# A language-model block on one core: TensorE takes the attention's units two at a time

## The chip, the cores and the metric

The kernel runs on one NeuronCore of a Trainium2 chip. The time is the device time of one execution in microseconds (us), from the chip. The median of three executions of the kernel before is 593.24 us (589.75 to 594.96). One further execution was profiled; it took 594.88 us.

## The reference

Rows of a table are gathered by token, an attention over each sequence is added, and then a mixture of experts:

```python
h = take(tok_weight, x)                      # x: 32 x 128 tokens, D = 256
X = layernorm(h)
q, k, v = X @ Wq, X @ Wk, X @ Wv             # 16 heads of 16
scores = where(causal, q @ k.T / 4, -inf)
h = h + (softmax(scores) @ v) @ Wo           # attention over 128 positions, all heads
X = layernorm(h)
top1 = argmax(softmax(X @ wg))               # 8 experts; capacity 641 rows each
y = gelu(X[slots] @ W1[e] + b1[e]) @ W2[e] + b2[e]     # 256 -> 1024 -> 256
h = h + where(valid, y[slot], 0) * weight_of_top1
```

All arrays are float32.

## The kernel before, in words

Two phases follow each other on the same core: attention with routing (to about 317 us of the profile), then the eight experts (to the end). The change is in the first.

**Groups and units.** The 32 sequences are taken in 16 groups of two (NG = 16, GB = 2). The attention of one group is eight units (UNITS = 8): a unit is four heads of one of the two sequences. For each unit there are, in this order: scores S (four 128 x 128 bf16 products, PE line 726, into bank S0 or S1 by the unit's parity), their row maxima on DVE (line 919, `mx`); once all eight maxima of a group are there, PE turns them (line 788, into bank M2), ACT negates them into `nm` (line 600) and sends them by a DMA (line 604) as one more row of `qs`; then the shifted scores C (four products with 97 contraction rows, line 739, into bank C0 or C1), the exponential on ACT (line 534, into `pt`, four buffers), the causal mask on POOL (line 479), and the values PV (line 833): eight matmul records, four heads in two passes each, each head in its own 32 columns of the array, into bank PV, which holds four units. ACT copies bank PV out after four units (`os`, line 544).

**Steps.** All engines go through 21 steps, i = 0 to 20, written out, with eight places s = 0 to 7 in each. Work of different groups overlaps by fixed lags: at place s the unit of S is (s - 12) mod 8, that of C (s - 23) mod 8, that of PV (s - 25) mod 8; so a unit's PV stands two places after its C. Besides these, some places hold other work, which the change calls `rest`:

- s = 1: projection Q of group i (`project`, twelve products, line 687), and ranks of the router (lines 810 to 814)
- s = 2: turn of `os` of the second sequence of group i - 4 (line 708, bank M1), projection K of group i (bank M2)
- s = 3: turn of `on` (line 629, bank M1), after DVE's division (lines 940, 942)
- s = 4: turn of the maxima of group i - 2 (line 788)
- s = 5: output projection O of group i - 4 (line 687, twelve products of 264 columns, banks M1 and M2); it waits for `otl` of DVE and, since it writes M2, for ACT's `nm`
- s = 6: turn of `os` of the first sequence of group i - 3 (line 708, bank M0)
- s = 7: value projection of group i, first sequence; turn of the normalised rows `xn` of group i + 1 (line 629, bank M0), which waits for DVE's division out of M0; value projection of the second sequence

At every place of step i the order on PE is: filler products (`idle_work`, only in a few steps at the start and the end), S, C, the rest, PV.

**Waits that matter.** S of unit u waits for the maxima of unit u - 2 (two S banks). C of unit u waits for the exponential of unit u - 2 (two C banks). C of a group's first unit (s = 7) waits for the DMA of `nm`. PV of unit u waits for the mask of unit u; the first PV of each four waits for the copy `os` of the four before.

**The other engines' order is written out too.** DVE: maxima of place s, then that place's other work: at s = 1 the ranks (`place`) and the rest of Q (`qr`, line 933), at s = 2 the division and the rest of K (`kr`, line 933, after ACT's copy of K, line 551), at s = 3 `otl`, at s = 5 the addition of O's result (line 977), the router's terms and the normalisation, at s = 6 a division and statistics. ACT: exponential of place s, then copies; at s = 4 the exponential, then `nm` and the issue of its DMA; at s = 5 the exponential, then `os`.

Of the kernel before, what the change touches and what calls it, by code (L numbers as in the profile page):

```python
# [35 lines left out]
UNITS = 8  # L36
# [25 lines left out]
def wait(engine, semaphore, value):  # L62

    if isinstance(value, int) and value <= 0:
        return
    engine.wait_ge(semaphore, value)
# [107 lines left out]
def attention_phase(nc, sb_in, sem, v):  # L174
    x, table, wq, wk, wv, wo, wg, b1, b2 = (v[n] for n in ("x", "table", "wq", "wk", "wv", "wo", "wg", "b1", "b2"))
    NB, S, D, E, H, DK, CAP, KC, GB, NG, GT, QUADS = (
        v[n] for n in ("NB", "S", "D", "E", "H", "DK", "CAP", "KC", "GB", "NG", "GT", "QUADS"))
# [3 lines left out]
    bS, bC, bPV, bM0, bM1, bM2 = (v[n] for n in ("bS", "bC", "bPV", "bM0", "bM1", "bM2"))  # L181
# [9 lines left out]
    with ExitStack() as scope:  # L191
# [96 lines left out]
        def group(n, off):  # L288

            if isinstance(n, int) and not 0 <= off < NG:  # L290
                return None
            return Turn(n, off, RING)
# [4 lines left out]
        def steps(eng, step):  # L297
            for i in range(LAST):
                step(0, i)
# [5 lines left out]
        def shift_unit(n, i, s, lag):  # L305

            d, u = divmod(s - lag, UNITS)
            return group(n, i + d), u
# [314 lines left out]
        def tensor(pe):  # L623
# [9 lines left out]
            def idle_work(bank, count):  # L633

                for _ in range(count):
                    pe.matmul(bank[:, :], trib[:, :], constb[:, :, :], start=True, stop=True)

            FILL = {(1, 1): 6, (1, 4): 32, (2, 6): 8, (NG + 3, 1): 4, (NG + 3, 3): 3, (NG + 3, 5): 6, (NG + 3, 6): 3,
                    (NG + 3, 7): 6, (NG + 4, 1): 2, (NG + 4, 6): 2, (NG + 5, 1): 4}
# [64 lines left out]
            def turn_values(dst, g, b):  # L704

                wait(pe, a_os, g.times(GB, b + 1))
                for a in range(QUADS):
                    last = pe.transpose(dst[:, a * P:(a + 1) * P], osb[b][:, a, :], identf[:, :])  # L708
                last.then_inc(pe_OT, 1)

            def step(n, i):
                for s in range(UNITS):

                    idle_work(bPV if i < NG else bS[0], FILL.get((i, s), 0))
                    g, u = shift_unit(n, i, s, S_LAG)
                    if g:
                        if u == 0:
# [10 lines left out]
                                             ks[g.slot][:, hh, b * S:(b + 1) * S], start=True, stop=True)  # L728
                        last.then_inc(pe_S, 1)

                    g, u = shift_unit(n, i, s, C_LAG)
                    if g:
                        if u == 0:
# [7 lines left out]
                                             qs[g.slot][0:KS_ROWS + 1, hh, b * S:(b + 1) * S], start=True, stop=True)  # L741
                        last.then_inc(pe_C, 1)

                    g = group(n, i - 4)
                    if g and s == 2:
# [69 lines left out]
                    if g and s == 6:  # L817
# [2 lines left out]
                        wait(pe, v_on, g.times(GB, -1))  # L820
                        turn_values(bM0, g, 0)

                    g, u = shift_unit(n, i, s, PV_LAG)
                    if g:
                        b = u // QUADS
                        if u == 0:
                            wait(pe, a_V[1], g.times(1, 1))
                        if u % QUADS == 0:
                            wait(pe, a_os, g.times(GB, b))
                        wait(pe, p_sel, g.times(UNITS, u + 1))  # L830
                        for j in range(4):
                            hh = (u % QUADS) * 4 + j
                            last = pe.matmul(bPV[32 * j:32 * j + 32, (u % QUADS) * S:(u % QUADS + 1) * S],  # L833
                                             va[g.slot][:, b, hh, :], pt[u % 4][:, j, :], start=True, stop=True)
                        last.then_inc(pe_PV, 1)

            steps(pe, step)
            idle_work(bS[0], 44)

        def vector(dve):  # L840
# [207 lines left out]
            steps(dve, step)  # L1048

        return {"sync": sync, "gpsimd": gpsimd, "scalar": scalar, "tensor": tensor, "vector": vector}  # L1050


# [332 lines left out]
```

## Time and profile before

| | |
|---|---|
| median of three executions | 593.24 us |
| profiled execution, its own time | 594.88 us |
| its span | 593.1 us |
| mean granted TensorE clock | 0.978 |
| busy: PE, PE weight loads | 546.1, 471.0 us |
| busy: DVE, ACT, POOL | 403.3, 341.8, 264.6 us |

Busy time is the union of an engine's instructions over the span; a matmul's end is modelled, so neighbouring matmuls overlap, and the distance from one start to the next says what one costs. A bracket after a row, `[0.21 <-issue]`, is the idle time of that engine before it and what ended it.

### The profile page before, as it was taken

Reading aid. Unit: us, or ns where it says so; the run is one execution under the profiler, and the core shown is the slowest. Engines: PE = TensorE matmul, PEld = TensorE weight load, DVE = VectorE, ACT = ScalarE, POOL = GpSimd, SP = SyncE. Lnnn points to the kernel's source line nnn. Section 1 sums busy time; section 2 is a strip of 40 time slices with the busy share of each in tenths; the row PEclk is TensorE's granted clock in tenths of the full one; section 3 lists DMA queues with packets and bytes.
Section 4 is the critical chain, followed back from the end, with each engine's and each line's share of the span. In section 5 each row is a group of like instructions: output and inputs, shape, how many; then the busy total and the mean of one; then the engine's idle time right before and its main releaser. Section 6 shows DMA issues by size and latency. Waiting matters only on the chain.

```text
span 593.1 us, 13953 instructions
## 1 busy us (share of the span) xinstructions
PE 546.1 (92%) x5067; PEld 471.0 (79%) x5067; DVE 403.3 (68%) x1076; ACT 341.8 (58%) x760; POOL 264.6 (45%) x345
## 2 busy tenths in 40 slices
PE   6875889999999999998888899999999999999991
PEld 3654677777888887775553799999999999999990
DVE  7554689989999999988546475757475655666511
ACT  3422566666666666665423684858484948484820
POOL 6634777777676767765534004040302122121212
PEclk9998999999999999999789899999999999999996
DMA  3799867777777777671112701615050606020100
GB/s 111 209 259 290 260 231 232 236 242 238 234 216 225 228 238 220 193 240 67 39 45 81 216 1 38 190 34 195 24 201 18 206 12 194 30 71 8 30 5 27
DMA packets 44612, 86.51 MB, mean 146 GB/s; under 512 B 7615, under 2 KB 33780, under 8 KB 40897
## 3 DMA queue, kind: packets, MB, share of 16 engines
q1 hardware_dynamic: 37632, 72.83, 39.9%
q0 software_dynamic: 6144, 12.67, 6.8%
q8 instruction: 41, 0.67, 0.5%
q10 hardware_dynamic: 768, 0.13, 0.1%
q14 instruction: 27, 0.21, 0.1%
HBM read 52.64 MB, written 31.74 MB: 142 GB/s over the span
## 4 chain that ended last, share of the span: by engine, by line
PE 76%; DVE 8%; DMA 6%; issue 4%; POOL 4%; ACT 1%; POOLq 0%; SPq 0%; ACTq 0%; DVEq 0%
PE M L687 13%; PE PV L1276 10%; PE S L1259 10%; PE C L1259 10%; PE M L1276 9%; PE PV L833 6%; PE S L726 5%; PE C L739 4%; PE M L629 3%; DMA ks<-k_parts 2%; PE C L1226 2%; PE M L708 2%; PE M L1214 2%; DVE mx L919 1%; DMA k_parts<-kp 1%
## 5 line engine op out<-in xcount | busy, mean ns | idle before, releaser
L1137 POOL DMA_INDIRECT out_dram<-ys,xs x48 | 50.7, 1057 | 212.7 <-DVE ys L1328 202.9
L534 ACT ACTIVATE pt<-C 128x512 f32<-128x512 f32 x128 | 76.3, 596 | 73.7 <-PE C L739 66.1
L479 POOL TENSOR_SCALAR_AFFINE_SELECT pt<-pt 128x512 f32<-128x512 f32 x128 | 81.2, 638 | 46.7 <-ACT pt L534 45.8
L919 DVE TENSOR_REDUCE mx<-S 128x4 f32<-128x512 f32 x128 | 86.4, 681 | 11.1 <-PE S L726 9.4
L1341 DVE TENSOR_TENSOR hl<-gl,hh 128x324 fp32r<-128x324 f32 x128 | 63.3, 495 | 38.9 <-ACT hh L1177 32.0
L1177 ACT ACTIVATE hh<-gl 128x324 fp32r<-128x324 f32 x128 | 60.8, 482 | 0.0
L833 PE MATMUL PV<-pt,va 128*32 128x128 f32 x1024 | 55.2, 289 | 4.6 <-issue 2.9
L726 PE MATMUL S<-ks,qs 128*128 128x128 bf16 x512 | 50.7, 223 | 8.4 <-DMA ks<-k_parts 5.3
L726 PEld LDWEIGHTS S<-ks,qs 128*128 128x128 bf16 x512 | 29.4, 98 | 32.6 <-issue 25.9
L739 PE MATMUL C<-qs,ks 97*128 97x128 bf16 x512 | 50.8, 222 | 1.8 <-DMA qs<-nm 1.8
L1328 DVE SCALAR_TENSOR_TENSOR ys<-C,xs 108x256 f32<-108x256 f32 x48 | 21.8, 481 | 40.2 <-PE C L1226 37.1
L1183 ACT ACTIVATE gl<-S,biases 128x324 f32<-128x324 f32 x64 | 34.5, 541 | 15.4 <-PE S L1259 12.5
L1293 DVE TENSOR_TENSOR wel<-w_raw,weh 128x512 fp32r<-128x512 f32 x64 | 40.9, 684 | 0.7 <-issue 0.7
L1259 PE MATMUL S<-xh,weh 128*128 128x324 f32 x128 | 41.2, 322 | 0.0
L1276 PE MATMUL M<-hh,weh 128*128 128x324 f32 x128 | 41.1, 321 | 0.0
L1276 PE MATMUL PV<-hh,weh 128*128 128x324 f32 x128 | 40.4, 316 | 0.0
L1259 PE MATMUL C<-xh,weh 128*128 128x324 f32 x128 | 40.3, 315 | 0.0
L1259 PE MATMUL S<-xl,weh 128*128 128x324 f32 x128 | 39.9, 312 | 0.0
L1276 PE MATMUL M<-hh,wel 128*128 128x324 f32 x128 | 39.9, 312 | 0.0
L1259 PE MATMUL C<-xl,weh 128*128 128x324 f32 x128 | 39.9, 312 | 0.0
L1276 PE MATMUL M<-hl,weh 128*128 128x324 f32 x128 | 39.9, 311 | 0.0
L1276 PE MATMUL PV<-hl,weh 128*128 128x324 f32 x128 | 39.8, 311 | 0.0
(170 smaller groups left out, 1617.1 us busy)
## 6 DMA issues: line engine op xcount, KB each, us to landing
w_raw<-in_L_ffn_W_dram SPq DMA_DIRECT2D x32, 512.0 KB, 7.4
qs<-q_parts SPq DMA_DIRECT2D x48, 256.0 KB
ks<-k_parts SPq DMA_DIRECT2D x48, 256.0 KB
q_parts<-qp SPq DMA_DIRECT2D x16, 384.0 KB
k_parts<-kp SPq DMA_DIRECT2D x16, 384.0 KB
rows_of_slots<-w_raw SPq DMA_DIRECT2D x6, 877.5 KB, 8.4
xs<-rows_of_slots SPq DMA_DIRECT2D x7, 658.1 KB
out_dram<-h SPq DMA_DIRECT2D x16, 256.0 KB, 7.0
```

The costliest lines, as they stand in the source:

```text
L479: pool.affine_select(out=buf[:, :, :], in_=buf[:, :, :], compare_op=ALU.is_ge, fill=0.0, base=0, pattern=[[0, 4], [1, S]], channel_multipl ...
L534: act.activation(pt[u % 4][:, :, :], bC[u % 2][:, :].rearrange("p (j t) -> p j t", j=4), ACT.Exp, scale=SCALE).then_inc(a_exp, 1)
L687: last = pe.matmul(dst, lhs[a](k), rhs[b](k), start=(m == 0), stop=(m == len(pairs) - 1))
L726: last = pe.matmul(dst[:, j * S:(j + 1) * S], qs[g.slot][:, hh, b * S:(b + 1) * S], ks[g.slot][:, hh, b * S:(b + 1) * S], start=True, stop ...
L739: last = pe.matmul(bC[u % 2][:, j * S:(j + 1) * S], ks[g.slot][0:KS_ROWS + 1, hh, b * S:(b + 1) * S], qs[g.slot][0:KS_ROWS + 1, hh, b * S: ...
L833: last = pe.matmul(bPV[32 * j:32 * j + 32, (u % QUADS) * S:(u % QUADS + 1) * S], va[g.slot][:, b, hh, :], pt[u % 4][:, j, :], start=True, ...
L919: dve.tensor_reduce(mx[g.slot][:, 4 * (u % QUADS):4 * (u % QUADS) + 4, u // QUADS], bS[u % 2][:, :].rearrange("p (j t) -> p j t", j=4), AX ...
L1137: pool.indirect_dma_start(out=outf, out_offset=bass.IndirectOffsetOnAxis(ap=xs[e.slot][:, j, D + 3:D + 4].bitcast(U32), axis=0), in_=ys[j] ...
L1177: act.activation(hh[:, f, cols], gl[u % 4][:, :], ACT.Copy).then_inc(a_hh, 1)
L1259: last = pe.matmul(up_bank[u % 4][:, 0:NH], w1[a][:, k, f * P:(f + 1) * P], xt[b][:, k, half * NH:(half + 1) * NH], start=(m == 0), stop=( ...
L1276: last = pe.matmul(down_bank[v % 2][:, 0:NH], w2[a][:, c, d * P:(d + 1) * P], ht[b][:, c, half * NH:(half + 1) * NH], start=(m == 0), stop ...
L1341: dve.tensor_tensor(hl[:, f, cols], gl[u % 4][:, :], hh[:, f, cols].bitcast(F32), ALU.subtract).then_inc(v_hl, 1)
```

## The change

On PE alone, the attention's places are taken two at a time. For s = 0, 2, 4, 6: PV of s - 1 and s, S of s and s + 1, C of s and s + 1, then the rest of s, and the rest of s + 1. PV of s = 7 of a step thereby falls to the head of the next step. The fillers of s stand ahead of the pair, those of s + 1 between the two rests. No other engine's program changes, and the waits of each piece stay as they are.

```diff
             def step(n, i):
-                for s in range(UNITS):
-
-                    idle_work(bPV if i < NG else bS[0], FILL.get((i, s), 0))
+                def scores(s):
+
                     g, u = shift_unit(n, i, s, S_LAG)
...
                         last.then_inc(pe_S, 1)
 
+                def shifted(s):
+
                     g, u = shift_unit(n, i, s, C_LAG)
...
                         last.then_inc(pe_C, 1)
 
-
+                def rest(s):
 
                     g = group(n, i - 4)
...
                         turn_values(bM0, g, 0)
 
+                def weighted(s):
+
                     g, u = shift_unit(n, i, s, PV_LAG)
...
                         last.then_inc(pe_PV, 1)
+
+                for s in range(0, UNITS, 2):
+                    idle_work(bPV if i < NG else bS[0], FILL.get((i, s), 0))
+                    weighted(s - 1)
+                    weighted(s)
+                    scores(s)
+                    scores(s + 1)
+                    shifted(s)
+                    shifted(s + 1)
+                    rest(s)
+                    idle_work(bPV if i < NG else bS[0], FILL.get((i, s + 1), 0))
+                    rest(s + 1)
```

## Rows read from the trace of the kernel before

**Rows 1.** Page's totals; window: PE, PEld, DVE, ACT, POOL (instructions), PEclk, DMA, GB/s.

```profile
PE 546.1 (92%) x5067; PEld 471.0 (79%) x5067; DVE 403.3 (68%) x1076; ACT 341.8 (58%) x760; POOL 264.6 (45%) x345
...
200.00:220.00 20.00, 19.96 (x259) 16.26 (x257) 18.51 (x60) 13.58 (x34) 14.29 (x20) 1.00 0.86 258
```

**Rows 2.** The chain of waits (start us, us, what): O of steps 4, 8, 15.

```profile
81.82 1.71 PE M L687 x12
...
147.83 1.69 PE M L687 x12
...
257.72 1.72 PE M L687 x12
```

**Rows 3.** Timeline of PE (start us, us), places 2 to 5 of a late step.

```profile
205.17 0.61 PE L708 MATMUL M<-identf,os 128*128 128x128 f32 x4
205.54 0.37 PE L687 MATMUL M<-xth,wh 128*128 128x256 f32 x1
...
206.92 0.28 PE L687 MATMUL M<-xth,wl 128*128 128x256 f32 x1
207.13 0.43 PE L833 MATMUL PV<-pt,va 128*32 128x128 f32 x8
...
207.73 0.39 PE L739 MATMUL C<-qs,ks 97*128 97x128 bf16 x4
207.95 0.61 PE L629 MATMUL M<-identf,on 128*128 128x128 f32 x4
208.49 0.43 PE L833 MATMUL PV<-pt,va 128*32 128x128 f32 x8
208.85 0.40 PE L726 MATMUL S<-ks,qs 128*128 128x128 bf16 x4
209.08 0.39 PE L739 MATMUL C<-qs,ks 97*128 97x128 bf16 x4
209.31 0.27 PE L788 MATMUL M<-identf,mx 128*32 128x128 f32 x1
209.51 0.43 PE L833 MATMUL PV<-pt,va 128*32 128x128 f32 x8
209.87 0.40 PE L726 MATMUL S<-ks,qs 128*128 128x128 bf16 x4
210.10 0.39 PE L739 MATMUL C<-qs,ks 97*128 97x128 bf16 x4
210.51 0.36 PE L687 MATMUL M<-wh,oth 128*128 128x264 f32 x1
...
211.93 0.28 PE L687 MATMUL M<-wh,otl 128*128 128x264 f32 x1
```

**Rows 4.** Timeline of PE where two PV groups are neighbours.

```profile
302.31 0.64 PE L833 MATMUL PV<-pt,va 128*32 128x128 f32 x16
```

**Rows 5.** Timelines of ACT and DVE in the same step.

```profile
207.24 0.60 ACT L551 ACTIVATE kp<-M 128x512 bf16<-128x512 f32 x1 [0.40 <-PE M L687]
209.64 0.60 ACT L534 ACTIVATE pt<-C 128x512 f32<-128x512 f32 x1
210.12 0.25 ACT L600 ACTIVATE nm<-M 32x128 bf16<-32x128 f32 x1
...
207.87 0.69 DVE L933 TENSOR_TENSOR kr<-M,kp 128x512 f32<-128x512 f32 x1 [0.48 <-ACT kp L551]
208.48 0.68 DVE L919 TENSOR_REDUCE mx<-S 128x4 f32<-128x512 f32 x1
```

**Rows 6.** Timeline of PE and its weight loads: the turn of xn, same step.

```profile
215.25 0.42 PEld L629 LDWEIGHTS M<-identf,xn 128*128 128x128 f32 x4 [0.21 <-issue]
215.29 0.63 PE L629 MATMUL M<-identf,xn 128*128 128x128 f32 x4
```

**Rows 7.** The issues of line 604 by line: time to landing.

```profile
DMA to landing us min/median/max: 1.8/1.8/3.5
```

## The prediction

> **What bounds the kernel now.** I read the totals first. PE is busy for 546.1 of 593.1 us, and in a late window of the attention for 19.96 of 20.00 us, with DVE at 18.51 beside it, ACT at 13.58 and POOL at 14.29; the granted clock there is 1.00 [rows 1]. So PE sets the pace and DVE is close behind: neither has more than about 8% to give.
>
> Second, the chain of waits gives the period of a step. The twelve products of the attention's output projection (called O here, once in a step, at s = 5) stand in it at 81.82, 147.83 and 257.72 us [rows 2]. Between the first two lie four steps (66.01 / 4 = 16.50 us each), between the last two seven (109.89 / 7 = 15.70 us each). These are the twelve steps i = 4 to 15 that have all their work.
>
> Third, PE in order of time through half a step [rows 3], with the distances from start to start. Values (PV) to scores (S): 208.49 to 208.85, 0.36 us, and again 209.51 to 209.87. S to shifted scores (C): 0.23. C to a transpose: 0.22. A group of four transposes to PV: 0.54, to projection products: 0.37. A projection's last product to PV: 0.21. Two PV groups stand side by side once, at the attention's end: sixteen products last 0.64 where eight last 0.43, so the second group starts 0.21 after the first [rows 3, 4].
>
> Fourth, what DVE and ACT do between these products [rows 5], since the new order changes how much PE has between giving work away and needing its result.
>
> **The change, part by part.** It adds and removes no instruction; every matmul, copy and DMA stays. ACT's, DVE's, POOL's and SP's programs are untouched. So nothing is to be priced but edges between kinds of work on PE, and waits.
>
> *Edges.* Of the eight PV groups of a step, four now follow another PV. Each such pair costs 0.21 instead of 0.36 once: 4 x 0.15 = 0.60. An entry into PV is saved as well: after transposes 0.54 - 0.37 = 0.17 (the pair at s = 6), after C about half of that, 0.09, an estimate between 0 and 0.17 (the pair at s = 0), and nothing after projection products [rows 3, 4]. S after S and C after C are taken at 0.22, an estimate from S to C and C to a transpose (0.23, 0.22): the same four products stream in each. Sum: **-0.85 us a step**. Bounds: -0.6 (no entry saved) to -1.3 (all four saved at 0.17). In one sentence apart: the Trainium skill, TensorEngine Tiling (Array Packing), Key Properties, says that changing the tiling mode drains TensorE, and PV alone works in 32-column tiles here. By that rule alone the change is a gain; the trace agrees on the drain (0.36 against 0.21).
>
> *The fifth S (s = 5).* It needs the maxima of the third, which DVE makes only after the rest of K, which waits for ACT's copy of K: the last K product starts at 206.92, K's copy at 207.24, the rest at 207.87, the maxima run to 208.48 + 0.68 = 209.16 [rows 3, 5]. That is 2.24 us after the last K product. Today PE fills 2.95 us until the S at 209.87 (PV, S, C, transposes of `on`, PV, S, C, the transpose of the maxima, PV), so nothing waits. In the new order S and C of s = 3 have gone ahead of K, and between K's last product and the S of s = 5 only the transposes of `on`, two PV and one S are left: 0.22 + 0.54 + 0.21 + 0.36 + 0.22 = 1.55. **PE waits 2.29 - 1.55 = 0.74 us**, with 0.05 for the signal (an estimate; from `nm` to O it is 0.14), and the C of s = 4 stands behind that S, though its own inputs are there.
>
> *O behind the negated maxima.* O writes bank M2 and so waits for ACT's copy `nm` out of it, and ACT takes that copy after the exponential of s = 4. From the C of s = 4 (209.08) the exponential ends at 210.24, `nm` at 210.37, and O starts at 210.51: 1.43 us [rows 3, 5]. Today there stand the transpose of the maxima, PV, S and C between, 0.23 + 0.20 + 0.36 + 0.23 + 0.22 = 1.24, so PE waits 0.19. In the new order PV and S of that place are gone ahead: C 0.22, transpose 0.23, O 0.20 = 0.65. **The wait grows from 0.19 to 0.78, +0.59.**
>
> *The turn of the next rows (s = 7).* It needs bank M0, which DVE leaves after adding O's result, the router's terms, the normalised rows, a maxima and a division: O's last product is at 211.93, the turn at 215.29, and PE (its weight loads) is idle for 0.21 ahead of it, so this DVE chain already ends last [rows 3, 6]. Its 3.36 us stay. PE's own work between is 3.15 and shrinks by the pair at s = 6 (0.15 + 0.17) to 2.83: **the wait grows by 0.32.** In other words that pair's saving is eaten on the spot.
>
> Sum: 0.74 + 0.59 + 0.32 - 0.85 = +0.80. Today's 15.70 holds some small waits which the new ones cover, so I take **+0.7 us a step** in the seven late steps: 4.9. Walking once round the loop gives much the same: K's end to maxima to S, C, exponential, `nm`, O, addition, turn, values, and again to K, 16.4 us against 15.70.
>
> *Five further places.* (a) The early steps already take 16.50, 0.8 more than the late ones, so they already wait for DVE and ACT; the new loop of 16.4 us would fit in. Between 0 and +0.7 each; I take 0.2, nearer to 0 since 16.4 is under 16.50: 4 x 0.2 = 0.8. (b) Step 16 has no Q and K but still `nm` before O: +0.6, from the same rows. (c) The first steps have no O; the S wait of 0.74 and the saving of 0.85 cancel; the first transpose of the maxima comes one S later, +0.3. (d) The PV of an even s now needs the mask of a C that is nearer: where Q stands between (0.23 + 0.22 + 1.38 and more) it is hidden, in the last three steps without Q it may wait some tenths, against savings of the same size: 0, bounds -1 and +2. (e) The first C of a group moves ahead of the transposes at s = 6 and of an S. It needs the transfer of `nm`, issued as `nm` is done at 210.37, while O starts at 210.51; the C comes 1.42 + 0.22 + 0.21 + 0.36 + 0.22 + 0.23 + 0.22 = 2.9 after O's start, 3.0 after the issue [rows 3, 5]. The transfer lands after 1.8 in the median and 3.5 at most [rows 7]: hidden mostly, 0 taken, bound +0.5 a step.
> The expert phase runs the same program from the same signals: 0.
>
> 4.9 + 0.8 + 0.6 + 0.3 = **+6.6 us**. The profiled execution took 594.88 us (span 593.1), 1.64 above the median of 593.24, so 601.5 there and **599.8** against the median. Bounds of this case: saving 1.3 instead of 0.85 in twelve steps gives up to 5 less, though only where it is not in front of one of the three waits (S and turn each swallow one pair); the C wait and the early steps at their ends give 6 more. So 594 to 606.
>
> **The rivals.** *A: the saving counts, the waits don't.* Place: the twelve full steps, where PE shows no idle time to speak of. Price: 12 x -0.85 = -10, and 583 in the end. For it: PE 19.96 of 20.00 [rows 1], and the rule above. Against: the three paths are measured, not assumed, and O and the turn wait already today (0.19 and 0.21). It decides if the three waits together grow by less than 0.85 a step instead of 1.65, that is, if signals or the DVE place (0.48 idle before the rest of K) come out half as long. *B: a draw.* Waits and savings within 0.3 of each other in the late steps, nothing in the early ones: 591 to 597, about 594. For it: PE and DVE were both near full, and both orders serve the same DVE program. *C: a further wait.* The transfer of `nm` at over 3 us in most steps, or an ACT queue in which the exponential of s = 5 slips behind its issue and holds back the copy that the PV of s = 5 needs: +0.5 to +0.8 a step more, 608. For it: that copy is due within 0.1 us of its use in my walk; against: DMA lands in 1.8. That the change doesn't do what it says cannot be: the order on PE is its text.
>
> A last sentence on rules: the Trainium skill, TensorE: Matmul & The Clock Gate, Step-by-step, says that matmuls stay in program order and only weight loads are pulled ahead; by it a waiting S holds back all that stands behind, as today's wait before O shows (0.19, worked out above).
>
> **Numbers.** Forecast case 0.55, A 0.17, B 0.15, C 0.13. This kernel's measurement can tell about 1% (5.9 us) from no change. The forecast case is centred on 599.8 with 599.2 as the border, so half of it is slower (0.3 with its upper tail), half within 1% (0.25). With C, slower 0.43; with B, same 0.40; A gives faster 0.17. The range leaves out A and the tail of C: 590 to 607.
>
> **What would show it.** In the late steps O to O 16.4 instead of 15.70. PV pairs of 0.64 for sixteen. PE idle before the S of s = 5, released by DVE's maxima, about 0.7; before O, released by ACT's `nm`, about 0.8; before the turn of xn, released by `on`, about 0.5; PE's busy time per 20 us down to some 18. DVE idle before the rest of K of 0.7 or more. The forecast is wrong if the period falls below 15.5, or if PV to PV takes 0.36 as PV to S does (then slower still), or if C shows DMA as its releaser.

## The result and the profile after

| | before | changed |
|---|---|---|
| median (4 executions each) | 592.11 us | 617.78 us |
| lowest to highest | 589.75 to 594.96 | 614.72 to 620.6 |
| profiled execution, its span | 594.88, 593.1 | 620.6, 618.9 |
| mean granted clock | 0.978 | 0.952 |

The ratio is 1.043, 95% interval 1.0384 to 1.0475: 4.3% slower. The direction was forecast; the size (+25.8 us of span, against +6.6) was not, and the time lies outside the range.

The totals of the changed kernel (page, part 1), and then its busy time in 20-us windows (PE, PEld, DVE, ACT, POOL with their instructions, then granted clock, DMA share, GB/s), early and late in the attention. They answer [rows 1].

```profile
PE 547.4 (88%) x5067; PEld 484.8 (78%) x5067; DVE 403.1 (65%) x1076; ACT 345.8 (56%) x760; POOL 264.6 (43%) x345
```

```profile
80.00:100.00 20.00, 16.75 (x201) 14.57 (x201) 15.50 (x46) 10.16 (x23) 13.55 (x18) 0.91 0.61 192
...
200.00:220.00 20.00, 18.59 (x255) 16.30 (x254) 18.09 (x59) 12.81 (x28) 12.63 (x19) 1.00 0.70 216
```

The busy totals have hardly moved; idle time has been added. O's start in each step, read from PE's timeline as in [rows 2], cuts the loss into stretches ("in the sum" is what the prediction took; a step is counted from its O to the next):

| stretch | before | changed | more | in the sum |
|---|---|---|---|---|
| start to O of step 4 | 81.82 | 83.91 | 2.1 | 0.3 |
| steps 4 to 8 | 66.0 (16.4, 16.4, 17.0, 16.3) | 75.0 (19.8, 19.8, 18.2, 17.1) | 9.0 | 0.8 |
| steps 8 to 15 | 109.9 (15.7) | 115.5 (16.3; the last 17.6) | 5.6 | 4.9 |
| steps 15 to 19 | 52.1 (13.5, 14.1, 13.2, 11.3) | 59.8 (17.0, 16.0, 14.1, 12.8) | 7.7 | 0.6 |
| O of step 19 to the end | 283.2 | 284.7 | 1.5 | 0 |

Two of the rows can't be put down to the order of the pairs. The way to O of step 4 takes between 80.4 (e9) and 86.1 us (e4, e16) in the experiments below. The way from O of step 19 to the end takes 282.8 to 283.8 in most of them and 284.8 to 285.0 in e4, e12, e14, e16 and e18, of which e12 and e18 are the kernel before but for small edits.

**Late steps** came out near the forecast (16.4 forecast, 16.3 measured). PE of the changed kernel in the half step that answers [rows 3] and [rows 6]:

```profile
204.16 0.66 PE L629 MATMUL M<-identf,on 128*128 128x128 f32 x4
204.74 0.64 PE L836 MATMUL PV<-pt,va 128*32 128x128 f32 x16
205.32 0.40 PE L725 MATMUL S<-ks,qs 128*128 128x128 bf16 x4
206.22 0.40 PE L725 MATMUL S<-ks,qs 128*128 128x128 bf16 x4 [0.50 <-DVE mx L934]
206.45 0.61 PE L740 MATMUL C<-qs,ks 97*128 97x128 bf16 x8
...
212.53 0.63 PE L629 MATMUL M<-identf,xn 128*128 128x128 f32 x4 [0.32 <-DVE on L957]
```

The pair of PV lasts 0.64 for sixteen, as in [rows 4]. The second S stands 0.90 after the first where 0.22 is its own length: it waits for the maxima, and C behind it. ACT and DVE in the same step, answering [rows 5]:

```profile
206.88 0.60 ACT L534 ACTIVATE pt<-C 128x512 f32<-128x512 f32 x1 [0.55 <-PE C L740]
207.37 0.25 ACT L600 ACTIVATE nm<-M 32x128 bf16<-32x128 f32 x1
...
204.87 0.69 DVE L948 TENSOR_TENSOR kr<-M,kp 128x512 f32<-128x512 f32 x1 [0.77 <-ACT kp L551]
205.48 0.68 DVE L934 TENSOR_REDUCE mx<-S 128x4 f32<-128x512 f32 x1
```

The chain of waits through this step (start us, us, what) shows what sets the period:

```profile
204.87 0.69 DVE kr L948
205.56 0.61 DVE mx L934
...
206.22 0.40 PE S L725 x4
206.61 0.24 PE C L740 x4
...
206.88 0.36 ACT pt L534
...
207.37 0.26 ACT nm L600
...
207.76 1.71 PE M L687 x12
...
210.52 0.65 DVE xn L898 x2
...
211.96 0.43 DVE on L957
...
212.53 0.63 PE M L629 x4
213.16 0.73 PE M L687 x6
213.89 0.57 PE PV L836 x16
214.46 0.55 PE S L725 x8
215.02 0.45 PE C L740 x8
...
219.08 1.44 PE M L687 x12
...
220.54 0.60 ACT kp L551
...
221.17 0.69 DVE kr L948
```

It is a loop through four instructions: the turn of `xn` (T), ACT's copy of K (k), DVE's rest of K (r), DVE's addition of O's result (h), and again T. I read their starts in every kernel; four links add up to the period. Any four instructions of a step would; what makes these a loop is that each waits for the one before or stands behind its engine's own work. ACT is idle before the copy of K until PE's product (0.70 in the changed kernel, 0.40 in [rows 5]), DVE before the rest of K until that copy (0.77 and 0.48), and PE or its weight loads before the turn (0.32 and 0.21). In between, DVE works without a marked gap in the kernel before; in the changed one it is idle once, 0.41 before h, for O's product.

| late step, us | T to k | k to r | r to h | h to T | sum |
|---|---|---|---|---|---|
| before | 7.6 to 7.8 | 0.61 to 0.63 | 4.4 | 3.04 | 15.63 to 15.81 |
| changed | 8.01 | 0.63 | 4.63 | 3.03 to 3.07 | 16.30 to 16.34 |

The last of the seven is 17.57, with an h to T of 4.30: there C of s = 7 waits 1.22 for the transfer of `nm`.

The kernel before ran round this loop too. Its PE looked full (19.96 of 20.00), and PE's work is the longest link (T to k), but PE was not the bound by itself: e7 below takes the waits before the second S out and PE's saving still doesn't come through.

**Early steps.** The timeline of POOL and PE of the changed kernel at the head of step 5, then windows of 2 us there (columns as above):

```profile
92.32 1.02 POOL L431 DMA_INDIRECT h<-in_L_tok_weight_dram,idt  x1 [0.19 <-issue]
93.64 0.95 POOL L431 DMA_INDIRECT h<-in_L_tok_weight_dram,idt  x1 [0.31 <-issue]
94.60 1.22 POOL L479 TENSOR_SCALAR_AFFINE_SELECT pt<-pt 128x512 f32<-128x512 f32 x2
...
93.30 0.43 PE L836 MATMUL PV<-pt,va 128*32 128x128 f32 x8
95.30 0.42 PE L836 MATMUL PV<-pt,va 128*32 128x128 f32 x8 [1.57 <-POOL pt L479]
95.66 1.03 PE L725 MATMUL S<-ks,qs 128*128 128x128 bf16 x8
```

```profile
92.00:94.00 2.00, 1.63 (x23) 1.26 (x21) 1.85 (x8) 1.80 (x6) 1.51 (x3) 1.00 0.97 385
94.00:96.00 2.00, 0.70 (x12) 0.51 (x13) 1.90 (x5) 0.17 (x1) 1.81 (x3) 0.91 0.71 242
96.00:98.00 2.00, 2.00 (x19) 2.00 (x17) 0.78 (x2) 0.84 (x2) 0.18 (x1) 0.50 0.05 16
98.00:100.00 2.00, 2.00 (x14) 2.00 (x13) 0.68 (x2) 0.27 (x1) 1.58 (x2) 0.73 0.00 0
```

PV of s = 2 now stands ahead of K and needs the mask of a C issued at the head of the step. That mask waits in POOL's queue behind a gather of the step before (a gather is two indirect DMAs, 1.0 us of POOL each). PE stands idle for 1.57 us, and after it the granted clock is 0.50, the level of 1.2 GHz: eight S products take 1.03 us instead of 0.62. The link T to k is 11.5 us in the two steps of 19.8 (8.3 to 8.9 before). The third of these steps is long for another reason: C of s = 7 waits 1.11 for the transfer of `nm`.

How much of this is the clock can be read in e6 (below), where the same wait stands in two steps in a row, once with the fall of the clock and once without:

```profile
94.33 0.47 PE L836 MATMUL PV<-pt,va 128*32 128x128 f32 x8 [1.57 <-POOL pt L479]
...
113.45 0.43 PE L836 MATMUL PV<-pt,va 128*32 128x128 f32 x8 [1.57 <-POOL pt L479]
```

```profile
96.00:98.00 2.00, 2.00 (x14) 2.00 (x13) 0.52 (x3) 1.11 (x2) 1.10 (x2) 0.50 0.04 12
...
114.00:116.00 2.00, 2.00 (x28) 2.00 (x26) 1.54 (x5) 1.12 (x2) 0.65 (x2) 1.00 0.48 166
```

The first of these steps takes 19.12 us, the second 17.56; T to k is 11.50 and 9.94. So the clock is worth 1.56 us of such a step, and the wait with the new order near K the other 1.2 over the 16.4 of before. The changed kernel has 0.68 more in r to h (4.63 against 3.95), which gives its 19.8.

**Last steps.** ACT and PE of the changed kernel at the head of step 16:

```profile
281.24 0.60 ACT L534 ACTIVATE pt<-C 128x512 f32<-128x512 f32 x1 [1.25 <-PE C L740]
281.73 0.48 ACT L579 ACTIVATE ex<-dl,h 128x8 f32<-128x8 f32 x2
282.11 0.58 ACT L544 ACTIVATE os<-PV 128x512 f32<-128x512 f32 x1
...
280.58 0.40 PE L725 MATMUL S<-ks,qs 128*128 128x128 bf16 x4 [0.18 <-DVE mx L934]
280.81 0.61 PE L740 MATMUL C<-qs,ks 97*128 97x128 bf16 x8
...
282.80 0.64 PE L836 MATMUL PV<-pt,va 128*32 128x128 f32 x16 [1.03 <-issue]
283.38 1.03 PE L725 MATMUL S<-ks,qs 128*128 128x128 bf16 x8
```

S of s = 1 waits 0.18 for the maxima, C of s = 0 stands behind it, its exponential follows C, and `os` stands behind this on ACT; PV of s = 1 needs `os`. In these steps there is no Q between C and the pair of PV, only five short products, so PE is idle for 1.03 us. The clock falls again: 0.50 in the windows from 284 to 290. Taken from O to O, the granted clock of these four steps is 0.80, 0.89, 0.74 and 0.77; it was 1.00, 0.94, 0.76 and 0.90 before.

### The profile page after: what moved, and what is told of

The parts are those of the page before. It is cut to its first block, busy times and chain, and to the rows that moved or that the text cites. A ratio compares the mean times of both kernels' runs of the same rounds, so it can differ in the third digit from the quotient of the medians.

```text
span 618.9 us, 13953 instructions
## 1 busy us (share of the span) xinstructions
PE 547.4 (88%) x5067; PEld 484.8 (78%) x5067; DVE 403.1 (65%) x1076; ACT 345.8 (56%) x760; POOL 264.6 (43%) x345
## 4 chain that ended last, share of the span: by engine, by line
PE 64%; POOL 9%; DVE 8%; DMA 7%; issue 6%; ACT 3%; POOLq 0%; SPq 0%; ACTq 0%
PE M L687 10%; PE S L1274 9%; PE M L1291 9%; PE PV L1291 9%; PE C L1274 9%; PE S L725 4%; PE C L740 3%; POOL h L431 3%; PE PV L836 3%; DVE mx L934 2%; POOL pt L479 2%; DMA qs<-nm 2%; POOL rows_of_slots L415 2%; PE M L708 2%; PE M L1229 2%
## 5 line engine op out<-in xcount | busy, mean ns | idle before, releaser
L534 ACT ACTIVATE pt<-C 128x512 f32<-128x512 f32 x128 | 74.5, 596 | 89.3 <-PE C L740 78.6
L479 POOL TENSOR_SCALAR_AFFINE_SELECT pt<-pt 128x512 f32<-128x512 f32 x128 | 80.4, 635 | 68.5 <-ACT pt L534 68.2
L725 PE MATMUL S<-ks,qs 128*128 128x128 bf16 x512 | 45.3, 230 | 17.6 <-DVE mx L934 10.5
L1192 ACT ACTIVATE hh<-gl 128x324 fp32r<-128x324 f32 x128 | 59.2, 469 | 0.0
L725 PEld LDWEIGHTS S<-ks,qs 128*128 128x128 bf16 x512 | 31.1, 102 | 33.5 <-issue 19.0
L836 PE MATMUL PV<-pt,va 128*32 128x128 f32 x1024 | 44.7, 288 | 10.8 <-POOL pt L479 5.5
L740 PE MATMUL C<-qs,ks 97*128 97x128 bf16 x512 | 43.5, 230 | 3.1 <-DMA qs<-nm 2.9
L836 PEld LDWEIGHTS PV<-pt,va 128*32 128x32 f32 x1024 | 24.4, 111 | 22.0 <-POOL pt L479 8.0
L1274 PE MATMUL S<-xh,wel 128*128 128x324 f32 x128 | 40.1, 313 | 0.0
L1291 PE MATMUL PV<-hh,wel 128*128 128x324 f32 x128 | 39.9, 311 | 0.0
```

The lines of the kernel that those rows point to most:

```text
L479: pool.affine_select(out=buf[:, :, :], in_=buf[:, :, :], compare_op=ALU.is_ge, fill=0.0, base=0, pattern=[[0, 4], [1, S]], channel_multipl ...
L534: act.activation(pt[u % 4][:, :, :], bC[u % 2][:, :].rearrange("p (j t) -> p j t", j=4), ACT.Exp, scale=SCALE).then_inc(a_exp, 1)
L725: last = pe.matmul(dst[:, j * S:(j + 1) * S], qs[g.slot][:, hh, b * S:(b + 1) * S], ks[g.slot][:, hh, b * S:(b + 1) * S], start=True, stop ...
L740: last = pe.matmul(bC[u % 2][:, j * S:(j + 1) * S], ks[g.slot][0:KS_ROWS + 1, hh, b * S:(b + 1) * S], qs[g.slot][0:KS_ROWS + 1, hh, b * S: ...
L1192: act.activation(hh[:, f, cols], gl[u % 4][:, :], ACT.Copy).then_inc(a_hh, 1)
L1274: last = pe.matmul(up_bank[u % 4][:, 0:NH], w1[a][:, k, f * P:(f + 1) * P], xt[b][:, k, half * NH:(half + 1) * NH], start=(m == 0), stop=( ...
```

## The experiments

All ratios are to the kernel before, run beside it, with 95% intervals. Steps are from O to O; "steps 4 to 8" are the four between the O of step 4 and that of step 8, "late" the seven after them, "last" the four after those. They are read from one profiled execution of each kernel.

**One half alone (e1, e2).**

```diff
 # e1: the loop over pairs
+weighted(s - 1); weighted(s)
+scores(s); shifted(s); rest(s); idle_work(...); scores(s + 1); shifted(s + 1); rest(s + 1)
 # e2
+scores(s); scores(s + 1); shifted(s); shifted(s + 1)
+rest(s); weighted(s); idle_work(...); rest(s + 1); weighted(s + 1)
```

> Only PV is paired (PV of s-1 and s at the head of the pair); S, C and the rest stay one place at a time, so the S wait on the late maxima is gone and the wait before O is about halved. Theory M (the missing 19 us come from the PV of an even s, whose mask is now too near behind its C: behind the gathers on POOL in steps 4 to 7, behind the exponential in the last steps, and the slower clock that the idle time brings): the mask is as near as in the changed kernel, so steps 4 to 7 stay at 18 to 20 us, the last steps stay long, only the late steps fall to about 15.3; ratio to before 1.02 to 1.03. Theory L (the loop maxima, exponential, nm, O is what costs, everywhere): ratio 1.00 or below.

> Only S and C are paired; each PV stays alone at the end of its place, as before. Theory M: PV has its old distance to its mask, so steps 4 to 7 take about 16.5 us and the last steps as before; the waits for the maxima (about 0.6) and for nm (about 0.4) stay and no edge is saved, so late steps take 16.3 to 16.5; ratio 1.01 to 1.015. Theory L: all the loss is here, ratio 1.04 or more.

Measured: e1 600.19 us, 1.0097 (1.006 to 1.0135); steps 4 to 8 16.95 three times and 16.5, late 15.3 to 16.1, last 14.2, 14.4, 13.6, 11.2. e2 613.51, 1.0273 (1.0207 to 1.0339); steps 4 to 8 16.6 to 17.0, late 16.4 to 16.7 but for one of 19.7 and one of 18.2, last 14.2, 15.6, 13.7, 11.9; T to k 8.04. More of the loss comes with S and C in pairs than with PV. In e2's two long steps C of s = 7 waits 1.80 and 1.78 for the transfer of `nm`, a wait that no late step of the kernel before shows.

Neither half has the 19.8. Theory M had the wait right and its price wrong: in e1 PV of s = 2 waits 1.38 for its mask, nearly as long as in the changed kernel (1.57), but the clock stays at 1.00 and the step takes 16.95. The step of 19.8 needs the wait and the fall of the clock after it.

**More room for the mask (e3, e4).**

```diff
 # e3, POOL
-                    if isinstance(n, int) and gathers and i and s in (6, 7):
+                    if isinstance(n, int) and gathers and i and s == 6:
 # e4: PV pair behind the two C
+scores(s); scores(s + 1); shifted(s); shifted(s + 1); weighted(s - 1); weighted(s); rest(s); ...
```

> The changed kernel with one gather of a group (two indirect DMAs) a step on POOL, at s = 6, in twelve steps instead of two a step (s = 6 and 7) in six. Theory M: POOL is free for the mask at the head of the next step, PV of s = 2 doesn't wait 1.6 us, the clock stays at 1.00 from 80 to 140 us, steps 4 to 7 fall from 19.8 to about 16.4; ratio 1.02 to 1.03. Theory L: nothing changes, 1.04.

> The changed kernel with the pair of PV behind the two C instead of ahead of the two S: the saving of the pairs is kept and PV's mask gets 0.9 us more. Theory M: steps 4 to 7 fall below 18 us, in the last steps each pair waits about 0.9 less; late steps stay at about 16.3, since the loop over maxima, exponential and nm doesn't run through PV; ratio 1.015 to 1.025. Theory L: 1.04 as before, or more, as S waits longer for the maxima.

e3: 616.54, 1.0355 (1.0295 to 1.0415). The first two of steps 4 to 8 fall from 19.8 to 16.45 and 16.47, with the clock at 1.00: the gather at s = 7 was the early loss, as expected. But the next two take 18.0 and 19.4 instead of 18.2 and 17.1, the late ones 16.9 to 17.6 instead of 16.3 and the last of them 18.5, and most is given back. Part of that is the transfer of `nm`, for which C waits 1.65, 1.24 and 1.59 in three of these steps. e4: 644.85, 1.0785 (1.0695 to 1.0875), late steps 18.4 and more. Theory M missed; theory L had "or more, as S waits longer". PE of e4:

```profile
189.39 0.50 PE L740 MATMUL C<-qs,ks 97*128 97x128 bf16 x4 [2.33 <-DMA qs<-nm]
...
203.16 0.40 PE L725 MATMUL S<-ks,qs 128*128 128x128 bf16 x4 [1.35 <-DVE mx L934]
```

With S and C one PV pair sooner after K and O, S waits 1.35 for the maxima (0.50 in the changed kernel), and C of s = 7 waits up to 2.33 for the transfer of `nm`.

**The two waits (e5 to e8).**

```diff
 # e5: C ahead of S
-scores(s); scores(s + 1); shifted(s); shifted(s + 1)
+shifted(s); shifted(s + 1); scores(s); scores(s + 1)
 # e6, DVE
+                maxima(3)
                 if g0:
                     rest_of(g0, bM2, kp, kr, a_k1, p_k3, v_kr)
-                maxima(3)
 # e7: both.  e8: the edit of e6 in the kernel before
```

> The changed kernel with the two C ahead of the two S of a pair. Theory B (in a pair the second S waits for DVE's maxima, and both C, whose inputs are there, stand behind it; from the late C come the late exponential, nm, mask, PV, and with the idle time the slow clock): C no longer waits, late steps fall from 16.3 to about 15.6 (0.74 less before O), steps 4 to 7 to 17.5 or less, the last steps by 1 each; ratio 1.01 to 1.02. Theory D (only the distance C to PV in PE's own work counts, 0.45 more here): late steps stay at 16.3; ratio 1.03 to 1.04.

> The changed kernel; DVE takes the maxima of s = 3 ahead of the rest of K, which it waits for today. Theory B: the S of s = 5 no longer waits (0.5 to 0.7), O comes as much sooner, late steps at 15.6 to 15.7; the steps at the head of which S waits for the maxima of s = 7 keep that; ratio 1.02 to 1.03. Theory D: late steps fall too, but steps 4 to 7 and the last ones stay; 1.03.

> Both edits together. Theory B: neither C nor the S of s = 5 waits; PE's saving of 0.85 a step shows, late steps at 15.0 to 15.4, ended by the DVE chain from O to the turn; ratio 0.98 to 1.00. Theory D: 1.02.

> Control: the kernel before with DVE's maxima of s = 3 ahead of the rest of K. There the S of s = 5 has 2.95 us of cover, so both theories expect 1.00 (0.995 to 1.01): the rest of K may come up to 0.3 later as S of s = 3 is issued late.

| | us | ratio | late steps | r to h | last steps |
|---|---|---|---|---|---|
| e5 | 606.27 | 1.0246 (1.0188 to 1.0304) | 15.8, three of 16.6 to 16.8 | 4.14 | 14.2, 14.8, 14.1, 11.8 |
| e6 | 606.96 | 1.0235 (1.0184 to 1.0286) | 15.62, the first 16.0 | 3.95 | 14.4, 17.2, 14.9, 11.8 |
| e7 | 602.21 | 1.0149 (1.0097 to 1.0201) | 15.62, the last 16.3 | 3.95 | 14.1, 15.8, 14.9, 11.5 |
| e8 | 596.12 | 1.0065 (1.0016 to 1.0115) | 15.77 | 3.85 | 13.5, 13.6, 12.4, 11.3 |

e5 and e6 came out as theory B said in the late steps: each edit is worth 0.5 to 0.7 a step (e5's three longer ones hold waits of 0.9 to 1.0 for the transfer of `nm`). But e7 did not get below e6, and its 1.0149 is above the 0.98 to 1.00 expected: neither C nor the second S waits there, and the loop still reads 8.01 + 0.63 + 3.95 + 3.04 = 15.63. The wait before O is not gone either; it is 0.59 in e6 and 0.7 in e7. Steps 4 to 8 are between 16.7 and 17.4 in e5 and e7, where the mask is waited for 1.2 and 1.3 us with the clock at 1.00. e8, the control, is slightly slower; its rest of K comes late (k to r 1.3), for the maxima that now stand ahead of it need the S of s = 3.

**ACT's queue, POOL's queue, the last steps (e9 to e12).**

```diff
 # e9 (on e7): PE turns the maxima right behind the PV pair of s = 4, and ACT:
+                if g2:
+                    wait(act, pe_mT, g2.times(1, 1))
+                    act.activation(nm[g2.slot][:, :], ...)
                 if g0:
                     second_part(g0, v_kr, kp, kr, a_k2)
                 scores(4)
 # e10 (on e9), e12 (on the kernel before), POOL
-... and s in (6, 7):
+... and s in (4, 6):
 # e11 (on e10): steps 16 to 20 one place at a time
+if i >= NG: scores(s); shifted(s); maxima_turned(s); rest(s); weighted(s)
```

> The kernel with C ahead of S and the maxima of s = 3 first, and now PE turns the maxima right after the PV pair of s = 4, and ACT copies nm ahead of the second part of K and of the exponential of s = 4. Theory B (order behind waiting work, on ACT as on PE): in that kernel the last link before O is ACT's queue (K's copy, exponential, oth, second part, exponential, nm: 3.15 us from K's end); it shrinks by 0.4 to 0.7, O waits 0.2 or less, late steps fall from 15.62 to 14.9 to 15.3; ratio 1.00 to 1.01 as the early and last steps keep theirs. Rival P (the period of 15.62 is DVE's own work plus its fixed chain, whatever PE does): 15.62 stays.

> The same, and POOL issues the two gathers of steps 1 to 6 at s = 4 and 6 instead of 6 and 7, so that none stands between a mask of an even place and the pair of PV that needs it first. Theory B: steps 4 to 7 fall from 17.1 to 16 or less, PE no longer waits for POOL at s = 2; ratio 0.3 to 0.8% below the kernel without it. Rival P: steps 4 to 7 stay at 17, as POOL's work is the same.

> The same, and steps 16 to 20, which have no projections to put between a C and its PV, take the places one at a time as the kernel before does. Theory B: the last steps fall from 14.1, 15.8, 15.0, 11.5 to the 13.5, 14.1, 13.2, 11.4 of before, -4; ratio to before 0.985 to 1.00, the first of these kernels not slower than before. If the loss at the end comes from elsewhere (the fillers, the clock), it stays.

> Control: the kernel before with the gathers at s = 4 and 6. There PV has more room behind the mask; all theories expect 0.995 to 1.005.

e9: 603.81, 1.0164 (1.0116 to 1.0211), late 16.07 (r to h 4.4): a miss, and in the late steps worse than e7 (the times of the two can't be told apart). e10: 606.11, 1.0185 (1.0132 to 1.0238), steps 4 to 8 17.3 to 17.8, where e9 has 17.2: a miss. e11: 602.69, 1.0135 (1.0074 to 1.0196), above the 0.985 to 1.00 expected; last steps 14.6, 13.6, 12.9, 11.6, 3.0 us less than e10. e12: 596.84, 1.0033 (0.9996 to 1.007), as expected, though its steps 4 to 8 take 67.8 us instead of 66.0. So a gather at s = 4 costs something in either order; that it delays other masks was not looked into. PE of e9 shows the miss:

```profile
196.43 0.27 PE L753 MATMUL M<-identf,mx 128*32 128x128 f32 x1 [0.49 <-DVE kr L952]
```

The turn of the maxima writes the bank of K and must wait for the rest of K; put ahead of C and S it holds those back, and the maxima of s = 4 and 5 on DVE with them. One more piece of work put ahead of ready work.

**K not behind the pair (e13 to e16).**

```diff
 # e13 (on the changed kernel), at s = 2
+weighted(1); scores(2); shifted(2); rest(2); weighted(2); idle_work(...); scores(3); shifted(3); rest(3)
 # e14 (on e13): C ahead of S in the pairs, DVE's maxima(3) ahead of the rest of K
 # e15 (on e14), e16 (on the changed kernel): steps 16 to 20 one place at a time
```

> The changed kernel with the pair at s = 2 taken one at a time, so that PV of 2, S of 3 and C of 3 stand behind K again instead of ahead of it. Theory R (all kernels so far go round one loop of four links: turn of xn to K's copy, K's copy to the rest of K, to the addition of O's result, to the next turn; late: before 7.6 + 0.6 + 4.4 + 3.0, changed 8.0 + 0.6 + 4.6 + 3.0): the first link falls to 7.3 to 7.4 (the pair at s = 0 keeps its saving), the third stays at 4.6 to 4.8; late steps 15.6 to 15.8; steps 4 to 7, where PV of 2 no longer stands ahead of K and waits for POOL, 17 or less; ratio 1.015 to 1.025. Rival W (the waits before S and O set the period, the place of K is no matter): S waits as before, late steps 16.3.

> The same, and C ahead of S in the pairs, and DVE takes the maxima of s = 3 ahead of the rest of K. Theory R: first link 7.35, third 3.95, late steps 7.35 + 0.63 + 3.95 + 3.04 = 15.0 unless DVE's own work of 14.9 ends it first; steps 4 to 7 about 16; ratio 0.995 to 1.005. Rival W: 15.62, as with K behind the pair.

> The same, and steps 16 to 20 one place at a time. Theory R and the runs on the last steps: 3 to 4 us less than without; ratio 0.985 to 1.00, the one of these kernels that may beat the one before.

> The changed kernel, steps 16 to 20 alone one place at a time. If the pairs cost the last steps what the trace shows (17.0, 16.0, 14.1, 12.8 against 13.5, 14.1, 13.2, 11.4), the time falls by 5 to 7.5; ratio 1.03. If it is the state in which step 15 leaves the engines, it falls by less than 3.

| | us | ratio | steps 4 to 8 | T to k, late | late |
|---|---|---|---|---|---|
| e13 | 608.09 | 1.0192 (1.012 to 1.0264) | 16.44, 16.45, 17.0, 17.9 | 7.85 | 16.3 to 16.6, the last 17.2 |
| e14 | 605.75 | 1.016 (1.0083 to 1.0237) | 16.5, 16.5, 16.8, 16.3 | 7.35 | 15.57, one 16.3, the last 16.6 |
| e15 | 599.65 | 1.0058 (1.002 to 1.0096) | 16.6, 16.3, 18.0, 16.3 | 7.38 | 15.59, three of 16.0 to 16.8 |
| e16 | 621.13 | 1.0421 (1.0354 to 1.0488) | 19.8, 18.2, 19.5, 18.4 | 8.47 | 16.9 to 18.6, the last 19.6 |

Early steps: e13 leaves POOL alone and only takes PV of 2, S of 3 and C of 3 from ahead of K; the two steps of 19.8 fall to 16.45. With e3 this settles what PE waits for: gather ahead of the mask, mask ahead of PV, PV ahead of K. e3 takes the first away and e13 the last, and the wait is gone. Late steps: e14's first link is the 7.35 that was forecast, but the maxima now stand ahead of the rest of K while S of s = 3 is late (k to r 1.29), and the sum is 7.35 + 1.29 + 3.89 + 3.04 = 15.57, not 15.0; its ratio of 1.016 is a miss too (0.995 to 1.005 expected). e13's first link was missed (7.85, not 7.35); PE is idle 0.4 there ahead of the PV of s = 1, which needs `os`. Last steps: e15 gains 1.0% on e14 (its four last steps sum to 52.1, as in the kernel before, where e14 has 57.7). e16 shows the same four at 54.3 instead of 59.8, 5.5 us less, but the kernel is no faster than the changed one: its seven late steps took 7.5 us more than those of the changed kernel. (The profiled execution of e16 was its slowest, 626.17 us; the others took 619.46 to 622.69.)

**A late exponential.** One cause of longer late steps is not a wait that the order of the program explains. PE and ACT of e16:

```profile
221.92 0.61 PE L740 MATMUL C<-qs,ks 97*128 97x128 bf16 x8
...
222.96 0.60 ACT L534 ACTIVATE pt<-C 128x512 f32<-128x512 f32 x1 [1.51 <-PE C L740]
```

The exponential starts 1.04 after its C; in the changed kernel it is 0.43 (214.85 to 215.28) in the same place. It is not ACT that is late: in both traces the exponential starts 0.02 or 0.03 after the semaphore event of its C, and it is this event that comes 0.63 after the modelled end of the products in e16 and 0.01 after it in the changed kernel. `os`, the copies of Q and of K follow on ACT. e13 has it in all late steps (1.03 to 1.30), e3 and e2 in two each, and e1 in five of seven, which lets it be priced. PE and ACT of e1, in a step of 16.0 and in one of 15.3:

```profile
171.47 0.39 PE L740 MATMUL C<-qs,ks 97*128 97x128 bf16 x4
203.42 0.39 PE L740 MATMUL C<-qs,ks 97*128 97x128 bf16 x4
...
172.69 0.60 ACT L534 ACTIVATE pt<-C 128x512 f32<-128x512 f32 x1 [1.47 <-PE C L740]
203.94 0.60 ACT L534 ACTIVATE pt<-C 128x512 f32<-128x512 f32 x1 [0.77 <-PE C L740]
```

The distance is 1.22 in the first and 0.52 in the second, and T to k is 8.0 and 7.56. The same 0.45 to 0.5 stands between e13 (7.85) and e14 or e17 (7.35), and between e16 (8.47) and the changed kernel (8.01). So e13's missed link and e1's longer late steps go with it: where it is absent, PV in pairs alone gives 15.3 us a step against 15.6 to 15.8 of before, as expected. ACT's program is the same in all of them. Why the event comes late in some kernels, no row says; it is open.

**What is left of the change (e17, e18).**

```diff
 # e17: pairs at s = 0, 4 (C, C, S, S) and 6 (S, S, C, C); s = 2, 3 and steps 16 to 20 one at a time
 # e18 (on the kernel before): in steps 1 to 15, ahead of the places 2 to 7
+weighted(0); shifted(0); shifted(1); scores(0); scores(1); rest(0); idle_work(...); rest(1); weighted(1)
```

> The changed kernel with s = 2 and 3 one at a time, C ahead of S in the pairs at s = 0 and 4 (S ahead at s = 6, where the C of s = 7 waits for nm's transfer), DVE's order as it was, steps 16 to 20 one at a time. Theory R: the links are 7.35 + 0.63 + 4.1 + 3.04 = 15.1 in late steps (before 15.7), steps 4 to 7 about 16.3; ratio 0.99 to 1.00. If the third link stays at 4.7 (nm), 15.7 and ratio 1.005.

> The kernel before with one pair a step, at s = 0 of steps 1 to 15: PV of 0 right behind PV of 7, then C, C, S, S, and the rest as before. Theory R: only the first link changes, 7.6 to 7.35, so late steps 15.45; the wait before O and the order at K stay; ratio 0.99 to 1.00 (3 us at most). If PE's order near K and O is no matter (theory W), the same.

e17: 598.03, 1.004 (1.0015 to 1.0064), the expectation's second case (1.005, third link not shortened); links 7.35 + 0.63 + 4.55 + 3.04 = 15.57, but four late steps of 15.9 to 16.3. e18: 595.54, 0.9997 (0.997 to 1.0024), as expected; late 15.4 to 15.6 (T to k 7.33 once, else about 7.5) and two of 16.2 (T to k 8.18). PE's saving of 0.25 in the first link is there in single steps and doesn't reach the end. No version beats the kernel before.

## Why the prediction was wrong

- **(a), (d) Early steps: the step that failed.** The prediction took 0.2 a step, 0.8 in all; measured were 9.0 over the four. Its reasons were that the new loop of 16.4 fits into the 16.50 of before, and in (d) that the mask of an even s is hidden where Q stands between C and PV. (d) looked only at PE's distance from C to PV. What the mask needs is its turn in POOL's queue, where two indirect DMAs stood ahead of it (1.3 us from start to start), and [rows 1 to 7] have no row of that queue. PE waited 1.57 us for it; e3 and e13 each remove the cause and the wait. Nor was the clock priced: the fall to 1.2 GHz over K is 1.56 us of such a step by e6. In the same steps the transfer of `nm` was waited for once (1.11).
- **(b), (d) Last steps: failed in the same way.** 0.6 forecast, 7.7 measured. (d) had seen that the PV of an even s isn't covered there, and took 0 for it. What waited was the PV of an odd s, behind the exponential and `os` on ACT (1.03), with the slow clock after it. e16 shows 5.5 us of the 7.7 to be the order of these steps, e15 against e14 the same (5.6); that all of it is this one wait is not shown.
- **"PE sets the pace"** was the wrong reading of a full PE. The period of before is the loop of four links; PE is the longest part of it. The forecast for the late steps held all the same, because the three waits were priced along that loop: 16.4 forecast, 16.30 measured. The 5.6 measured against the sum's 4.9 holds 1.2 that the sum had at nothing, the transfer of `nm` at the last of these steps; without it the loss is 4.4.
- **Edges: right.** PV pair 0.64 for sixteen (0.21 for the second), S to C in a pair 0.45 for two groups (0.22 taken each). The Trainium skill, TensorEngine Tiling (Array Packing), Key Properties, says that changing the tiling mode drains TensorE; the trace agrees: 0.36 against 0.21. The saving exists and is paid away.
- **The three waits of a late step: right in kind and about in size.** Before S at s = 5: 0.74 forecast; 0.50 idle on PE, 0.68 between two S starts above their own length. Before O: 0.78 forecast; 0.59 on PE, 0.79 on its weight loads. Before the turn: 0.5 forecast; 0.32 on PE, 0.50 on the weight loads. e6 removes the first; the second stays in e6 (0.59) and e7 (0.7). That they can't simply be added to PE's saving is what e7 shows: with the first wait gone and the saving kept, the step is 15.62 and not 15.0. The loop says it better: three groups more ahead of K (+0.2 to 0.4 in T to k, the saved edges taken off), S and C late behind the rest of K (+0.2 in r to h), and nothing in h to T.
- **(c) First steps:** 0.3 against 2.1; the trace has an S wait of 1.11 and a PV wait for `os` of 2.25 (1.28 before), with a clock of 0.77 to 0.92 from 50 to 80 us. Not tried by itself, and kernels with other small edits differ as much there, so the cause is open. The same holds of the 1.5 behind step 19.
- **(e) The transfer of `nm`:** 0 taken, bound +0.5 a step. The bound held here (1.22 once in seven late steps), but it is the wait that comes back in e2 to e5 and e14 to e17: the pairs have moved C of s = 7 up to it.
- The mechanism of rival C (a further wait) was the right kind with the wrong place. Its 608 and the range's 607 were both too low, since (d)'s bound of +2 came from no row.

## What to carry to other kernels

When work on an in-order engine is grouped, list for each item that moves ahead what it waits for, through every queue to its start (POOL and ACT too, with what else stands there), and what ready work comes to stand behind it. A PE at 99.8% busy may still be on a loop with two other engines: follow one period of the chain of waits and add up its links before you call a saving on PE a gain. When you price a new wait of PE, price the slower clock that may follow it as a term of its own, with its own chance: here the same wait of 1.57 us cost 1.56 us more with it than without.

## What the runs showed of the hardware

- From the start of a PV group (eight products, in 32-column tiles) to the next PV group it is 0.21 us, to full-width work 0.36 us. From four transposes to a PV group it is 0.17 more than from four transposes to projection products.
- After 1.57 us of idle PE, with further gaps around it, the granted clock read 0.50 in the window of 2 us that followed and 0.73 in the one after; a run of eight S products took 1.03 instead of 0.62. The next such wait of e6 (1.57), and those of e1 (1.38) and e7 (1.27), left the clock at 1.00.
- An indirect DMA holds POOL's queue: about 1.0 us each, 1.3 from start to start, with the masks behind it.
- PE's semaphore event for a finished group can come later than the group's modelled end: 0.01 in the changed kernel, 0.63 in e16 at the same place, and ACT follows it by 0.02. e16 and the changed kernel differ only in the order of the last steps; in the late steps, where e16 has this event late, T to k is 8.47 against 8.01 and a step 16.9 or more against 16.3. Why is open.
